# Layer 3 of a four-layer attention and feed-forward kernel: sums before the next maximum, queries made by quarters

## The reference

```python
def _L2_xattn_ref(query, key, value, Wq, Wk, Wv, Wo):
    q = (query @ Wq).reshape(b, sq, NUM_HEADS, HEAD_DIM).transpose(0, 2, 1, 3)
    k = (key @ Wk).reshape(b, sk, NUM_KV_HEADS, HEAD_DIM).transpose(0, 2, 1, 3)
    v = (value @ Wv).reshape(b, sk, NUM_KV_HEADS, HEAD_DIM).transpose(0, 2, 1, 3)
    k, v = jnp.repeat(k, rep, axis=1), jnp.repeat(v, rep, axis=1)
    scores = jnp.einsum('bhqd,bhkd->bhqk', q, k) * HEAD_DIM ** (-0.5)
    probs = jax.nn.softmax(scores, axis=-1)
    out = jnp.einsum('bhqk,bhkd->bhqd', probs, v)
    return out.transpose(0, 2, 1, 3).reshape(b, sq, DIM) @ Wo
...
x = x + _L1_ffn_ref(_layernorm(x), ...)     # codes of four bits: f1
x = x + _L2_xattn_ref(_layernorm(x), ctx, ctx, ...)
x = x + _L2_ffn_ref(_layernorm(x), ...)     # router and 64 small experts: f2
```

## Time and profile before

| | |
|---|---|
| median of three runs | 1646.39 us |
| the profiled execution's own time | 1643.18 us |
| its span | 1641.4 us |
| TensorE busy, mean granted clock | 1548.2 us (94%), 0.992 |
| VectorE, ScalarE, GpSimd busy | 830.9, 757.8, 519.6 us |

### The profile page before, as it was taken

One profiled execution on the slowest core, in us unless ns is written; L12 is line 12 of the kernel. 1 busy time (PEld: TensorE's weight loads), 2 busy tenths in 40 slices (PEclk: granted clock), 3 DMA queues, 4 the chain that ended last, 5 costly groups with the idle time before them and its releaser, 6 DMA issues. The chain is left out here.

```text
span 1641.4 us, 26020 instructions
## 1 busy us (share of the span) xinstructions
PE 1548.2 (94%) x9532; PEld 1266.2 (77%) x9538; DVE 830.9 (51%) x1703; ACT 757.8 (46%) x2535; POOL 519.6 (32%) x648
## 2 busy tenths in 40 slices
PE   8898997799999999999999998879999999999998
PEld 6777776688888888889889886646455577888876
DVE  4666675454444554554444436765565321343465
ACT  4455455354544545445455555444343211454552
POOL 7667663322212222222222223333232000123323
PEclk9999999999999999999999999998999999999999
DMA  8000001011010100101010110001000001122101
GB/s 244 8 7 8 8 1 40 26 59 39 27 39 27 39 27 27 36 4 39 27 40 26 40 52 1 29 5 53 34 1 0 22 8 44 42 73 75 50 26 61
DMA packets 44414, 58.05 MB, mean 35 GB/s; under 512 B 25472, under 2 KB 32656, under 8 KB 41472
## 3 DMA queue, kind: packets, MB, share of 16 engines
q1 hardware_dynamic: 43872, 56.05, 10.8%
q10 hardware_dynamic: 352, 0.34, 0.1%
q0 software_dynamic: 64, 0.00, 0.0%
HBM read 48.77 MB, written 2.10 MB: 31 GB/s over the span
## 5 line engine op out<-in xcount | busy, mean ns | idle before, releaser
L1797 ACT ACTIVATE big<-pb 128x128 f32<-128x128 f32 x384 | 106.6, 278 | 310.6 <-PE pb L848 201.9
L2163 POOL TENSOR_TENSOR big<-big 128x512 f32<-128x512 f32 x96 | 100.0, 1042 | 260.2 <-DVE big L1438 260.2
L1848 ACT ACTIVATE big<-pb,big 128x128 f32<-128x128 f32 x384 | 136.1, 368 | 64.9 <-issue 41.9
L1433 DVE TENSOR_REDUCE big<-pb 128x4 f32<-128x512 f32 x96 | 65.9, 686 | 181.3 <-PE pb L887 173.7
L863 PE MATMUL pb<-wkh,CXh 128*128 128x256 f32 x512 | 149.0, 291 | 1.5 <-DVE big L1423 1.5
L2153 POOL TENSOR_SCALAR big<-big 128x6 f32<-128x6 f32 x64 | 13.2, 206 | 418.5 <-ACT big L1797 418.2
L863 PE MATMUL pb<-wkl,CXh 128*128 128x256 f32 x512 | 144.3, 282 | 0.0
L863 PE MATMUL pb<-wkh,CXl 128*128 128x256 f32 x512 | 143.7, 281 | 0.0
L1221 DVE TENSOR_TENSOR X<-X,pb 128x512 f32<-128x512 f32 x128 | 87.0, 679 | 85.4 <-PE pb L1069 41.5
L912 PE MATMUL pb<-woh,oh 128*128 128x512 f32 x256 | 111.8, 437 | 8.2 <-DVE X L1221 5.0
L848 PE MATMUL pb<-wqh,CXh 128*128 128x512 f32 x256 | 101.9, 398 | 5.8 <-DVE big L1403 4.4
(11 more groups left out here) (277 smaller groups left out, 3975.3 us busy)
## 6 DMA issues: line engine op xcount, KB each, us to landing
big<-in_w SPq DMA_DIRECT2D x17, 1024.0 KB, 4.9
big<-in_w SPq DMA_DIRECT2D x24, 256.0 KB, 2.9
big<-in_w SPq DMA_DIRECT2D x8, 512.0 KB, 3.4
o<-o SPq DMA_DIRECT2D x96, 32.0 KB, 1.9
X<-in_x SPq DMA_DIRECT2D x8, 256.0 KB, 5.1
big<-in_cn SPq DMA_DIRECT2D x8, 256.0 KB, 2.9
CXlf<-in_cT SPq DMA_DIRECT2D x8, 256.0 KB, 5.2
big<-in_wa SPq DMA_DIRECT2D x1, 2048.0 KB, 8.1
```

Source lines behind the costliest of these rows:

```text
L1433: v.tensor_reduce(m[j % 2], quarters(bank(p)), AX, MAX, negate=True).then_inc(S.m, 1)
L1797: y = a.activation(sq[i % 2], bank(p)[:, j * width:j * width + 128], ACT.Square, accum_out=ss[i % 2][:, first + j:first + j + 1])
L1848: y = a.activation(e_[:, c], bank(p)[:, c], ACT.Exp, bias=m[j % 2][:, k:k + 1], scale=1.0, accum_out=z[j % 2][:, k:k + 1])
L2163: g.tensor_tensor(quarters(e_), quarters(e_), bc(r[j % 2], 128), MUL).then_inc(*on.to(S.pn))
```

## The change

Three things move. In `pipe2` the entry l2_z stands ahead of l2_s, so that VectorE sums batch u - 3 before it takes the maxima of batch u - 2; GpSimd's division moves in its own queue in the same way. l2_q is cut into 16 quarters, one for each round: two stand in step 1 ahead of f1's part, two behind it, then one in each step from 2 to 9, two in step 10 and two in step 12. And l3_load stands behind step 13. Each quarter is one use of the shared banks, so the banks of all later stages move on.

```diff
     def queries_at(u):
-        return {1: 0, 3: 1, 6: 2, 9: 3}.get(u)
+
+        return {1: [2, 3], 2: [4], 3: [5], 4: [6], 5: [7], 6: [8], 7: [9], 8: [10], 9: [11], 10: [12, 13],
+                12: [14, 15]}.get(u)
...
-                             ("l2_v", 5, every), ("l2_t", 4, every), ("l2_s", 2, every), ("l2_z", 3, every),
+                             ("l2_v", 5, every), ("l2_t", 4, every), ("l2_z", 3, every), ("l2_s", 2, every),
...
             if name == "ffn1":
+                if step == 1:
+                    order.extend(("l2_q", j) for j in range(2))
                 run(1, ffn1)
+            elif name == "l2_q":
+                order.extend((name, j) for j in i)
...
-        if step == 10:
+        if step == 13:
             order.append(("l3_load", 0))
...
-    if stage == "l2_q":
-        return [(r, sh) for r in range(4)]
-    if stage in ("l2_a", "l2_v", "l2_c", "f2_turn", "f2_a", "f2_o", "l3_turn"):
+    if stage in ("l2_q", "l2_a", "l2_v", "l2_c", "f2_turn", "f2_a", "f2_o", "l3_turn"):
         return [("p", sh)]
...
-            def l2_q(n):
+            def l2_q(j):
+                n, r = divmod(j, 4)
+                p = PSUM["l2_q", j, "p"]
                 lt_ready("l2", 2 * n)
                 lt_ready("l2", 2 * n + 1)
                 on.wait_ge(D.w2q, 16)
-                for r in range(4):
-                    p = PSUM["l2_q", n, r]
-                    on.wait_ge(p.free, p.n)
-                    for c in range(4):
-                        a = pe.matmul(bank(p)[:, 0:256], w2q[:, c, r, :], x_tiles(LT, c, 2 * n, 2),
-                                      start=(c == 0), stop=(c == 3))
-                    a.then_inc(p.full, 1)
+                on.wait_ge(p.free, p.n)
+                for c in range(4):
+                    a = pe.matmul(bank(p)[:, 0:256], w2q[:, c, r, :], x_tiles(LT, c, 2 * n, 2),
+                                  start=(c == 0), stop=(c == 3))
+                a.then_inc(p.full, 1)
...
             def l2_s(b):
-                q = PSUM["l2_q", b // 4, 3]
+                q = PSUM["l2_q", b // 4 * 4 + 3, "p"]
```

More of the change, by code:

```diff
@@ L659, in lt_user @@
         def lt_user(kind, t):
-            return {"l1": None, "l2": ("l1_k", 56 + t, "p"), "f2": ("l2_q", t // 2, 3), "l3": ("f2_h", t, 1),
+            return {"l1": None, "l2": ("l1_k", 56 + t, "p"), "f2": ("l2_q", t // 2 * 4 + 3, "p"), "l3": ("f2_h", t, 1),
                     "f3": ("l3_q", 26 + t // 4 * 4, "p")}[kind]
@@ L1907, in l2_kv, with l2_q @@
                 y.then_inc(p.free, 1)
-            def l2_q(n):
-                read = PSUM["l1_k", 8 * NT - 1, "p"]
+            def l2_q(j):
+                (n, r), p, read = divmod(j, 4), PSUM["l2_q", j, "p"], PSUM["l1_k", 8 * NT - 1, "p"]
                 on.wait_ge(read.full, read.n + 1)
[L1912 to L1918, removed]
+                on.wait_ge(p.full, p.n + 1)
+                rows = q2_rows(4 * n, r // 2)
+                a.activation(view(rows, r % 2 * 64, [[256, 2], [4096, 2], [1, 64]]),
+                             bank(p)[:, 0:256].rearrange("p (t b q) -> p t b q", t=2, b=2), ACT.Copy,
+                             scale=0.25).then_inc(p.free, 1)
             def l2_e(b):
@@ L2344, in l3_load @@
             def l3_load(_):
-                q = PSUM["l2_q", 3, 3]
+                q = PSUM["l2_q", 15, "p"]
                 on.wait_ge(q.full, q.n + 1)
```

## The result

The kernel after took 1629.99 us (median of four runs, 1627.85 to 1630.52), the kernel before in the same comparison 1646.51 (four runs, 1645.98 to 1650.64): ratio 0.9887, 95% interval 0.987 to 0.9903.

A forecast was written before the change was run, and what follows sets the result against it. TensorE was taken as the bound except in layer 3's steps 0 to 9, held by a softmax ring. Steps 13.5 us, less 1.5 for the clock, plus 0.5 behind, gave 12.5 us: 1633.9 us from 1646.39, range 1630 to 1643.

The forecast's parts named there:

- the table of steps: Layer 3, steps 0 to 9: each step the longer of TensorE work and ring; router product at 1127.1 us before clock deduction.
- The ring: Layer 3's softmax: scores, maximum, exponentials repeat every 5.2 us in place of 8.2, sums and division no longer in it.
- the wait for the division: Sign in layer 3's first stretch: turning's wait for GpSimd's division falls from 8.6 us to under 2.
- late sums: Rival: in every step VectorE's sums come after the scores end, 1.75 us onto the ring; gain 3.8, 1642.6 us; chance 0.11.
- a ScalarE bound: Rival: ScalarE's order makes five thin steps 1.3 us longer each, 6.5 of 12.5 us go; 1640.4 us; chance 0.12.
- the lead lost behind the stretch: Rival: expert chains of VectorE and ScalarE set steps 10 to 21, end moves 1 us or less; 1645.5 us; chance 0.08.
- the slower rival: TensorE stays at 1.2 GHz through layer 3's thin steps, 35 us more; 1669 us; chance 0.07.
- One such stretch: Low-clock deduction in layer 3's steps: 0.94 us on batch 2's scores, 0.6 on what follows, 1.5 us; bounds 0 and 9.
- between 0 and that I take 0.5: Behind the first stretch: turnings no longer waiting for the division win 0.5 us, bounded by TensorE's 1.63 us idle there.
- as long as now plus 7 us: Sign: the stretch behind the router product lengthens by 7 us, the full length of the four query quarters moved there.
- the median shown, 1646.39, lies 3.2 above it and becomes 1633.9: Whole kernel: profiled execution goes from 1643.18 to 1630.7 us, and the median stays 3.2 us above the profile.
- a spread of 1 us between executions: Whole kernel: allowance at the range's low end, below 1631.3 us with both open terms good, giving 1630.

The follow-up runs named there:

- e3: The kernel before with only the order changed (l2_z ahead of l2_s), queries still in four lumps, load behind step 10: 1636.58 us, ratio 0.9945 to before.
- e4: The kernel after with l2_s and l2_z back in the old order, so only the query quarters and later load: 1636.82 us, ratio 0.9963 to before.
- e9: The kernel before with only l3_load moved behind step 13: 1644.75 us beside 1644.77 for before, ratio 1.0002.
- e2: The kernel after, unchanged, run and profiled again: 1628.29 us, ratio 0.9912 to before.
- e10: The kernel after, unchanged, run again in a later comparison: 1630.74 us, ratio 0.9911 to before.
- e13: The kernel before, unchanged, profiled again: execution of 1645.58 us, V turn at 1064.93 us.
- e14: The kernel before, unchanged, profiled again: execution of 1649.57 us, V turn at 1070.33 us.
- e1: The kernel before, unchanged, run and profiled again: 1643.87 us beside 1643.93, ratio 0.9996.
- the combined version: The kernel after with batch 0's V turn ahead of step 0 and f1's last tile four steps later: 1625.19 us, again 1627.82 us.
- e6: The kernel after with batch 0's V turn (l2_a) moved ahead of step 0: 1631.31 us, ratio 0.9909 to before.
- e12: The kernel after with batch 0's V turn ahead of step 0 and f1's last tile four steps later, second run: 1627.82 us, ratio 0.9893 to before.
- e5: The kernel after with a query quarter moved from step 5 to step 3: 1628.69 us, ratio 0.9898 to before.
- e7: The kernel after with f1's last tile four steps later and its queries in steps 12 and 13: 1628.61 us, ratio 0.9894 to before.

## Why the prediction was right, and where it was wrong

**Right: the mechanism and the table of steps.** Six of the seven distances between scores came out within 0.2 us of the working; 2 to 3 is the one that didn't. The ring of "5.2 us in place of 8.2" is 5.5 where TensorE's work is longer than the ring; batches 0 and 1 did not move against the V turn; the scores of batch 2 are 26.36 us behind it (26.5 forecast), the router product 65.74 (65.5 with the deduction for the clock). e3 and e4 show that both moves were needed, and e9 that the load costs nothing. One sign missed: the wait for the division was to fall to under 2 us and fell to 3.0, though the working itself had a gap of 2.8 us there. Of the rivals, late sums and a ScalarE bound would have shown as steps longer than the table's; the lead lost behind the stretch would have left the 578 us as they were; the slower rival wanted a low clock through the thin steps, where the whole stretch has 0.95.

**Right within its bounds, but small: the clock.** "One such stretch", 1.5 us: batch 2 to 3 took 1.95 us more than the 5.4 of the working in after, and 3.0 in e2 and e10 (8.38, 8.44). The router product came 65.74, 66.76 and 66.84 us behind the V turn, 66.4 on the mean, where the five profiles of before have 84.8; with the 6.9 us of quarters still to come the steps won 11.4 us, where 12.0 was forecast.

The forecast, 1633.9, is 3.9 us above the measured time. By the figures below 1.3 us of this lie in the sum and 2.6 in the time that it was taken from.

**Wrong: "between 0 and that I take 0.5"**, the term behind the stretch. It measured 1.9 us (e3: 1.93 with no quarters; after: 6.9 - 4.99). I had bounded it by TensorE's idle time there, 1.63 us, as a sum of what TensorE lost. But the records of a group overlap: a turning matmul is recorded as 0.27 us and eight of them as 1.09 together, so a short wait inside the group counts as busy for the most part. The second half of the turning waited for the division in a group that reads 1.41 in place of 1.09, and the scores for the masking behind it. So the idle time was no upper bound, and the prediction's own check, "as long as now plus 7 us", failed: it is plus 4.99. Of the 1.9 only 0.8 shows as idle time (1.63 before, 0.85 after). In e4, with the old order, the 1.9 is not won: two of the four waits for the division are there (7.27 us from scores to scores), and at the other two places, where the quarters stand, the projection waits for a V copy (10.61 in place of 10.24).

The Trainium skill ("Perfetto Trace Analysis", Identifying the Most-Contended Engine) judges TensorE's headroom by the share of its weight loads, or by MFU (its arithmetic as a share of the peak), which I have not worked out. By the first nearly half of that stretch would be free, as loads are busy for 79.75 of 147.41 us. The trace disagrees: in e4 the four quarters moved there lengthen it by 6.7 us, and their own work is 6.9.

**Wrong: "the median shown, 1646.39, lies 3.2 above it and becomes 1633.9"**, with "a spread of 1 us between executions" at the low end. The 3.2 us are no property of the layers but of where the V turn comes, and that varied from 1062.80 to 1070.33 in one program. Before's four runs, 1645.98 to 1650.64, have the times of e13 and e14 rather than of its profile; after's four were 1627.85 to 1630.52, with its profile the slowest. (That they differ ahead of the V turn is argued from the five profiles; before's four runs have no trace, and of after's only the slowest has one.) Means from the V turn: before 578.1, after 564.3, so 13.8 us of the 16.5 are the change's, and I put the other 2.7 down to the draw of executions. (In e2 and e10's comparisons the medians are 15.6 and 14.0 apart; over all 48 runs of before in the comparisons and all 15 of after they are 1645.1 and 1630.0, 15.1 apart.) The gain of 13.8 was in "9 to 15"; the 1 us at the range's end was too little where single executions of before go from 1641.4 to 1651.2.

The sum in terms: steps 12.0 forecast, 11.4 measured; behind 0.5 forecast, 1.9 measured; together 12.5 and 13.3. The 0.5 missing to 13.8 lies behind the 87th addition, where executions differ by more than that: from it to the end the profiles of before take 302.5 to 304.1 us and those of after 302.2 to 303.4 (a wait of TensorE for a DMA of the output is 1.9 us in before, 0.5 in e1, 0.6 in after, 1.7 in e10).

**Left open.** Why the clock of the first 60 us differs between executions. Whether before's four runs really lost their time ahead of layer 3. Whether the combined version's 3 to 5 us show in medians.

## What to carry to other kernels

In a softmax whose engines take their work in order, put the sums of a batch ahead of the next batch's maximum, and the filler matmuls one to a step: the first was worth 9.5 us here, the second 6.3, both 13.8. Bound what an order can win by start-to-start times between groups and by the waits of the weight loads, not by idle time alone, since most of a short wait inside a group reads as busy. Compare kernels from a fixed event ahead of the change to the end: that repeated to within 1.8 us here, while whole executions of one kernel spread over 10 us.

## What was not expected of the hardware

- Executions of one program differ ahead of layer 3 by up to 7.5 us (V turn 1062.80 to 1070.33). The late one has a granted clock of 0.89 in the first 60 us (e6 and e12 too), the early ones 1.00.
- Filling a gap of TensorE ahead of a group need not give that group full speed: e5's scores at 1089.98 stand behind 1.15 us of idle time and still take 2.08 us (the clock at 1.2 GHz), while e7's at 1079.35, behind 1.42, take 1.13.
